# Moving the normalisation of the context tiles from VectorE to GpSimd

## The reference

```python
def _ln(x):
    mu = jnp.mean(x, axis=-1, keepdims=True)
    var = jnp.var(x, axis=-1, keepdims=True)
    return (x - mu) * jax.lax.rsqrt(var + LN_EPS)
```

## Time and profile before

| | us |
|---|---|
| median of 3 runs | 4722.28 |
| lowest, highest | 4713.96, 4735.18 |
| the profiled execution | 4714.82 |
| its span on the core | 4713.1 |
| VectorE busy in the span | 3582.4 |
| TensorE busy | 3444.2 |
| ScalarE busy | 2859.7 |
| GpSimd busy | 612.9 |

### The profile page before, as it was taken

The page is one execution under the profiler, slowest core; times in us unless marked ns, Lnnn a source line. Parts: engine busy times, 40 slices in busy tenths (PEclk is TensorE's granted clock), DMA queues, the critical chain, the costliest instruction groups (busy, mean ns, idle before and its releaser), DMA issues. The chain is left out here.

```text
span 4713.1 us, 74839 instructions
## 1 busy us (share of the span) xinstructions
PE 3444.2 (73%) x28020; PEld 1497.4 (32%) x28020; DVE 3582.4 (76%) x5514; ACT 2859.7 (61%) x5351; POOL 612.9 (13%) x1338
## 2 busy tenths in 40 slices
PE   2669999976789999848466666666566656579987
PEld 2223333332323333323132223223232222235543
DVE  6658889826578888436799999999999999732223
ACT  1456888843547878627377777777776776621223
POOL 1122122001324232003011010101000000000000
PEclk7798999986879999968577767777777777789999
DMA  4553343205533342045211010101111110000000
GB/s 135 146 132 93 85 112 86 51 22 160 122 88 96 88 102 67 17 119 124 70 40 40 22 39 22 39 22 39 27 34 32 25 21 11 3 29 28 21 0 9
DMA packets 277494, 285.16 MB, mean 61 GB/s; under 512 B 38800, under 2 KB 246040, under 8 KB 276248
## 3 DMA queue, kind: packets, MB, share of 16 engines
q1 hardware_dynamic: 277144, 280.53, 23.6%
HBM read 152.08 MB, written 127.18 MB: 59 GB/s over the span
## 5 line engine op out<-in xcount | busy, mean ns | idle before, releaser
L1312 ACT ACTIVATE prob<-xa_ps 128x512 f32<-128x512 f32 (+1 forms) x2880 | 1563.4, 597 | 409.5 <-PE xa_ps L1207 385.8
L1399 DVE TENSOR_REDUCE mpart<-ring 128x1 f32<-128x400 f32 (+2 forms) x2816 | 1294.4, 526 | 285.6 <-PE ring L1155 282.3
L1155 PE MATMUL ring<-k_st,q_st 52*128 52x400 bf16 (+2 forms) x3584 | 863.9, 371 | 364.0 <-ACT s_sb L1294 315.4
L1226 PE MATMUL xa_ps<-prob,va 128*16 128x256 f32 (+1 forms) x9984 | 852.0, 424 | 0.5 <-ACT prob L1312 0.5
L1207 PE MATMUL xa_ps<-q_st,k_st 55*128 55x256 bf16 x5504 | 623.0, 300 | 58.2 <-ACT prob L1312 44.1
L1202 PE MATMUL xa_ps<-neg_id,un 128*128 128x128 bf16 (+1 forms) x3328 | 365.0, 276 | 361.7 <-ACT prob L1312 359.9
L1285 ACT ACTIVATE un<-s_sb 128x1601 fp8e4<-128x1601 f32 x256 | 392.8, 1536 | 344.4 <-DVE s_sb L1425 344.4
L1155 PEld LDWEIGHTS ring<-k_st,q_st 52*128 52x128 bf16 x3584 | 254.5, 100 | 888.2 <-ACT s_sb L1294 394.0
L1294 ACT ACTIVATE s_sb<-ring 128x400 f32<-128x400 f32 (+1 forms) x1024 | 471.9, 524 | 31.8 <-PE ring L1155 23.4
L1425 DVE MATCH_REPLACE8 s_sb<-m8b,s_sb 128x1601 f32<-128x1601 f32 x256 | 478.8, 1946 | 0.0
L1418 DVE MATCH_REPLACE8 s_sb<-mpart,s_sb 128x1601 f32<-128x1601 f32 x256 | 478.7, 1945 | 0.0
(11 more groups left out here) (227 smaller groups left out, 3370.5 us busy)
## 6 DMA issues: line engine op xcount, KB each, us to landing
k_st<-kc_dram SPq DMA_DIRECT2D x192, 300.2 KB, 5.4
o_dram<-o_sb SPq DMA_DIRECT2D x192, 128.0 KB, 1.9
kc_dram<-k SPq DMA_DIRECT2D x72, 300.0 KB, 3.4
q_st<-q_dram SPq DMA_DIRECT2D x80, 192.0 KB, 4.0
kc_dram<-k SPq DMA_DIRECT2D x72, 200.0 KB, 3.8
ctx_t<-in_ctxT SPq DMA_DIRECT2D x16, 800.5 KB, 4.8
k_st<-k_dram SPq DMA_DIRECT2D x48, 192.0 KB, 5.0
kc_dram<-k SPq DMA_DIRECT2D x24, 300.8 KB, 3.3
```

The lines of the kernel that those rows point to most:

```text
L1155: nc.tensor.matmul(ring_ps[:, r % BANKS, 0:w], q_st[rows, b % NQ, 2 * t + pl, qt * P:(qt + 1) * P], k_st[rows, slot_of(n), pl, c0:c0 + w], ...
L1226: last = nc.tensor.matmul(av_ps[32 * k:32 * k + VW, n % 2, :], va[0:sizes[j], b % NVB, j, G * t + k, :], prob[0:sizes[j], s % NPROB, (2 * ...
L1312: nc.scalar.activation(prob[0:size, s % NPROB, hf * 512:(hf + 1) * 512], x_ps[0:size, (2 * s + hf) % XBANKS, :], ACT.Exp, scale=HEAD_SCALE ...
L1399: nc.vector.tensor_reduce(mpart[:, n % 4, row, c:c + 1], ring_ps[:, r % BANKS, 0:chunks[c][1]], AX.X, ALU.max).then_inc(g["red"].sem, 1)
```

## The change

The 13 normalising instructions of each batch leave VectorE's stream and stand in GpSimd's, behind its three memsets, with the same operands and operations. GpSimd waits for the root of the batch. VectorE goes from the reciprocal of batch b to the statistics of batch b+1. From b = 2 on these wait until GpSimd has normalised batch b-2, where they waited for its root. The code of TensorE, ScalarE and SyncE is as it was.

```diff
@@ stage_context_norm
             pool.wait_ge(loaded.sem, loaded.at(3))
+            for b in range(B):
+                k = b % 2
+                pool.wait_ge(rstd_r.sem, rstd_r.at(b + 1))
+                for j in range(NT):
+                    last = nc.gpsimd.tensor_scalar(raw[:, k, j, :], raw[:, k, j, :], mv[:, k, j, 0:1], rstd[:, k, j:j + 1],
+                                                   ALU.subtract, ALU.mult)
+                last.then_inc(norm_r.sem, 1)
 
         @block.vector
         def _(dve):
...
                 if b >= 2:
-                    dve.wait_ge(rstd_r.sem, rstd_r.at(b - 1))
+                    dve.wait_ge(norm_r.sem, norm_r.at(b - 1))
...
                 nc.vector.reciprocal(rv[:, k, :], rv[:, k, :]).then_inc(ve_r.sem, 1)
-                dve.wait_ge(rstd_r.sem, rstd_r.at(b + 1))
-                for j in range(NT):
-                    last = nc.vector.tensor_scalar(raw[:, k, j, :], raw[:, k, j, :], mv[:, k, j, 0:1], rstd[:, k, j:j + 1],
-                                                   ALU.subtract, ALU.mult)
-                last.then_inc(norm_r.sem, 1)
```

## The result

The changed kernel takes 4770.8 us (median of 4 runs, 4768.2 to 4773.7) where the kernel before took 4728.7 us in the same comparison: a ratio of 1.0093, 95% interval 1.0065 to 1.0122. It is 42 us slower. The median of the kernel before rests on 4 runs here; 39 further runs of it, which the experiments are compared with, have medians of 4722.9 (19 runs) and 4721.9 us (20 runs), and against these the change would cost 48 to 49 us. The interval, 31 to 58 us, holds both. The profiled execution took 4768.3 us, its span 4766.4. The forecast was 4731 us, no change that can be told, and the range ended at 4763; both missed.

A forecast was written before the change was run, and what follows sets the result against it. The stage was held bound by the ring of two raw buffers, not VectorE. 90.0 + 26.0 = 116.0 us against 107.4 is 8.6 us later; on the median 4722.3 this gave 4731 us, range 4714 to 4763.

The forecast's parts named there:

- The closed ring of a buffer: Normalising stage: normalisation, transposes and copies, store, load, statistics and root follow without slack, 19.02 us a turn before the change.
- Nothing gained by freeing VectorE: Normalising stage: early statistics end in a wait of ScalarE, whose root follows the copies; overlap won 0.3 us, once.
- 90.0 + 5N: End of the last normalisation in us, one batch's normalisation time counted five times; 116.0 us forecast, against 107.41 before.
- N: Time in which one batch is normalised: 3.42 us on VectorE, forecast 5.2 us on GpSimd, break-even 3.48 us.
- 66.4 + 8N: End of the last normalisation in us from N = 7.9 on; 148.0 us at N = 10.2.
- thirteen like a two-input operation: GpSimd's normalisation of one batch: each instruction priced at 0.458 us, 0.398 start to start, 5.2 us for thirteen.
- the other chain of the prediction: Normalising stage: root, GpSimd, TensorE and copies run one batch after another, seven legs of 4.0 + N, from N = 7.9.
- case of dear columns: Rival, GpSimd's normalisation: per-partition columns fetched as separate small reads, 0.84 us an instruction; + 40.6 us, 4763 us; chance 0.27.
- VectorE's statistics and GpSimd do not hinder each other: Rival denied here: odd batches' statistics and even normalisations shut each other out, 3.6 us each, 23 in all, 4745 us; chance 0.05.
- the change did not do what it says: Rival denied here: root not behind the copies, batch 6 to 7 some 7 us, loss 6 us; no separate chance given.
- Anything else (a granted clock that differs later on): Rival, outside the other cases: something else, such as a different granted clock later in the kernel; no size; chance 0.03.
- the prediction's own sign (stages behind this one differ by more than a few us): Stages behind about 124 us: the prediction is wrong if they differ by more than a few us.

The follow-up runs named there:

- three_buffers: The kernel before (normalisation on VectorE) with three buffers of raw in place of two, first three loads issued together; 4712.0 us, 0.9977 of before.
- two_wide: The changed kernel with GpSimd normalising each batch in two instructions over all 13 tiles, a subtraction and a product; 4739.2 us, 1.0034 of before.
- root_first: The changed kernel with ScalarE taking the root of batch b+1 ahead of the copies of batch b; 4764.5 us, 1.0087 of before.

## Why the prediction failed

**What bounds the stage: right.** The closed ring of a buffer, VectorE not being the limit, and 3.7 us from the end of a normalisation to the last copy (after: 48.65 to 51.56 + 0.77 = 52.33) all hold. `three_buffers` confirmed it: next stage at 103.6 us with VectorE's work unchanged.

**Nothing gained by freeing VectorE: right.** The root of batch 1 came directly behind the copies of batch 0 (52.21), 10 us after VectorE's reciprocal. Hand-over and root together were put at 0.3 us; the trace has 52.52 - 52.33 = 0.19.

**The formulas: right.** 90.0 + 5N for a small N was met by `two_wide` within 0.2 us. For N over 7.9 the prediction gave 66.4 + 8N, which is 147.1 at N = 10.09; measured 146.39, the difference being seven hand-overs of 0.1 us less.

**The step that failed is the price of GpSimd's instruction.** The step is "thirteen like a two-input operation: 12 x 0.398 + 0.458 = 5.2 us", the term N of the sum. The prediction read it off the nearest rows, two-input work, and took the row with more operands as the nearer. One instruction takes 0.792 us, start to start 0.776, and N = 10.1. Two parts were wrong: the price itself, and the 0.06 us by which an instruction was to start before the one ahead ends (0.016 here). The two-input row was no upper end: this instruction has a slope of its own, 3.3 ns an element against 2.1 there, and two columns on top. From N = 7.9 on the other chain of the prediction decides, so 4.9 us more in N became some 30 us more in the stage (154.5 against the 124 us of the forecast).

With 10.1 in place of 5.2 the prediction's own case of dear columns follows (N = 10.2, + 40.6 us; measured 42). That it met the time so closely was in good part luck. It put a column at 0.19 us and nothing else; start to start 0.38 us were missing (0.776 against 0.398), and the columns make 0.17 of them. The rest is the slope (1.2 ns x 128 = 0.15) and some 0.06 of fixed part. I gave that case 0.27, of which 0.16 for N above 8.1 us, and the rule against it (a second read costs 12 ns at 8 elements) compared operations on whole tensors and said nothing on columns. That half of VectorE's speed would give the loss that I forecast was also loose: it gives N = 6.8 us, an estimated loss of 17 us by 90.0 + 5N, and not 8.6. The trace shows a factor of three (0.776 against 0.257 us).

**The range** ended at that case's 4763 us with nothing beyond it. It was built on a median of 4722.3 for the kernel before; with the fourth run that median is 4728.7, and 42 us on top lie outside; on the old median they would still end at 4764. The 4714 to 4735 us of the runs were counted at the lower end, but not at the upper.

**The chances** of no change that can be told (0.80) failed with N. The other rivals stand as they were weighed: VectorE's statistics and GpSimd do not hinder each other (two normalisations side by side do, by 5 to 11% behind batch 0, but the change has none such), the set-up instruction hid under its cover (the first normalisation starts 0.20 us after the root ends at 38.35, against 0.09 in batch 1), and the change did not do what it says, since no earlier normalisation came of it. "Anything else (a granted clock that differs later on)" had 0.03. In the two profiles it is there: 13 of the 14 us outside the stage lie in the last stretch, at a lower clock. By the prediction's own sign (stages behind this one differ by more than a few us) that is a miss; over the ten profiled executions this stretch takes 659 to 674 us, in no clear order of the stage's length.

## What to carry to other kernels

Before work is moved off a busy engine, ask what its completion waits for: here VectorE's reciprocal was ready 10 us before anyone could use it, since the next consumer in ScalarE's stream stood behind the old batch. Turning two instructions of such a stream around can exchange one wait for another (`root_first`); write down what each of them waits for, the loads included. A price for an instruction that the trace does not show is not bounded by other kinds of instruction on that engine; an upper end needs a wide margin, and the range must be carried past it. And when two profiles differ by more than the stage that was edited, find where in the span the rest lies before it is called scatter.

## What the runs showed of the hardware

- GpSimd, 128 partitions, f32: `tensor_scalar` with two operations and two columns takes 0.35 us + 3.3 ns an element (0.776 us at 128, 1.20 at 256, 2.05 at 512); a `tensor_tensor` whose second operand is a column spread over 13 tiles takes 1.8 ns an element (2.97 us at 1664). For the same result two of the second kind cost 6.0 us, thirteen of the first 10.1.
- A column in place of a number costs GpSimd 0.084 to 0.086 us each.
- VectorE and GpSimd normalising side by side in SBUF slow each other: ten of VectorE take 2.81 us against an estimated 2.66, nine 2.65 against 2.39; three of GpSimd take 2.51 against an estimated 2.34, four 3.28 against 3.12. In batch 0 GpSimd's are slower still (2.82 and 3.59). Statistics of VectorE beside GpSimd's work are slowed by nothing that can be seen (thirteen take 2.55 to 2.61 us after the change, 2.61 before).
- The last 660 us of the kernel, the same 2107 TensorE instructions in every run, took 659.5 and 661.6 us at a granted clock of 0.91, 665.7 to 668.5 at 0.90, 672.8 at 0.89 and 674.4 at 0.88.
